# Cross-attention energies split to high and low float16 in SBUF and turned by DMA transposes instead of TensorE, with new instruction orders

## What is computed

```python
x = layernorm(x + causal_attention(x))        # 16 heads of 32
query = ctx @ Wq.T + bq                       # ctx (4, 512, 256), 128 wide
key = ctx @ Wk.T + bk
attention = softmax(query @ key.T, axis=-1)   # (512, 512) for each batch
x = layernorm(x + einsum('bln,bmn->blm', x, attention))
x = layernorm(x + ternary_gated_ffn(quantised(rms_norm(x))))   # hidden 2048
```

## Time and profile before

| | us |
|---|---|
| median of 3 runs | 647.17 (646.59 to 647.51) |
| span of the profiled execution, its own time from first to last instruction | 649.9 |
| TensorE busy | 610.3 |
| VectorE busy | 527.2 |
| ScalarE busy | 417.9 |
| GpSimd busy | 340.8 |

### The profile page before, as it was taken

The page is one execution under the profiler, slowest core; times in us unless marked ns, Lnnn a source line. Parts: engine busy times, 40 slices in busy tenths (PEclk is TensorE's granted clock), DMA queues, the critical chain, the costliest instruction groups (busy, mean ns, idle before and its releaser), DMA issues.

```text
span 649.9 us, 14332 instructions
## 1 busy us (share of the span) xinstructions
PE 610.3 (94%) x5356; PEld 417.1 (64%) x5356; DVE 527.2 (81%) x1376; ACT 417.9 (64%) x789; POOL 340.8 (52%) x472
## 2 busy tenths in 40 slices
...
DMA packets 31461, 45.63 MB, mean 70 GB/s; under 512 B 5664, under 2 KB 22560, under 8 KB 29856
## 3 DMA queue, kind: packets, MB, share of 16 engines
...
...
## 4 chain that ended last, share of the span: by engine, by line
PE 62%; DVE 11%; ACT 6%; issue 4%; SPq 1%; POOL 1%; DMA 1%; POOLq 0%; ACTq 0%; DVEq 0%
PE ps_b L672 20%; PE ps_b L840 15%; PE ps_b L855 14%; PE ps_b L767 4%; PE ps_b L746 3%; PE ps_b L776 2%; DVE ps_b L1118 1%; PE ps_b L729 1%; ACT ph L949 1%; PE ps_b L725 1%; SPq L634 1%; ACT ps_b L950 1%; DVE qk L1100 1%; ACT p L936 1%; DVE dg L1211 1%
## 5 line engine op out<-in xcount | busy, mean ns | idle before, releaser
L1118 DVE CUSTOM_DVE_ANT_0 ps_b<-ps_b,future 128x256 f32<-128x256 f32 (+3 forms) x256 | 118.9, 515 | 17.7 <-PE ps_b L725 11.3
L1319 POOL TENSOR_TENSOR ph<-p,ph 128x512 f16<-128x512 f32 x96 | 110.3, 1165 | 42.2 <-ACT ph L873 41.5
L840 PE MATMUL ps_b<-xqT,sg 128*128 128x256 f16 x1024 | 124.3, 275 | 3.8 <-ACT xqT L873 2.4
L855 PE MATMUL ps_b<-sd,hp 128*128 128x512 fp8e4 x512 | 119.1, 379 | 0.0
L1315 POOL TENSOR_TENSOR hp<-gt,hp 128x512 f16<-128x512 f32 x64 | 74.1, 1164 | 82.7 <-ACT hp L873 82.7
L840 PEld LDWEIGHTS ps_b<-xqT,sg 128*128 128x128 fp8e4 x1024 | 99.4, 98 | 22.5 <-issue 4.1
L1277 POOL TENSOR_SCALAR_AFFINE_SELECT p<-p 128x256 f32<-128x256 f32 (+1 forms) x96 | 46.5, 494 | 77.8 <-ACT p L936 77.0
L672 PE MATMUL ps_b<-xhl,wh 128*128 128x256 f16 x480 | 82.4, 273 | 0.0
L855 PEld LDWEIGHTS ps_b<-sd,hp 128*128 128x128 f16 x512 | 48.7, 98 | 51.1 <-POOL hp L1315 0.3
L1028 ACT ACTIVATE gt<-gt 128x512 f32<-128x512 f32 x64 | 40.1, 629 | 47.0 <-DVE gt L1226 46.9
L936 ACT ACTIVATE p<-ps_b 128x512 f32<-128x512 f32 x96 | 54.2, 598 | 19.3 <-PE ps_b L746 18.5
...
## 6 DMA issues: line engine op xcount, KB each, us to landing
st<-qk SPq DMA_DIRECT2D x192, 64.0 KB, 2.0
...
out_dram<-rows SPq DMA_DIRECT2D x16, 256.0 KB, 2.0
xin<-in_xT_dram SPq DMA_DIRECT2D x14, 256.0 KB, 3.5
...
hp<-in_wT_dram SPq DMA_DIRECT2D x4, 256.0 KB, 4.4
```

The costliest lines, as they stand in the source:

```text
L840: ins = pe.matmul(ps[:, a * HALF:(a + 1) * HALF], sg[:, ("gg", "uu").index(name), c, ht * P:(ht + 1) * P], xqT[:, c, :], start=c == 0, sto ...
L855: ins = pe.matmul(ps[:, :], hp[:, (UNITS * s + n) % HP_SLOTS, h, a, t * P:(t + 1) * P], sd[:, ht, :], start=ht == h == 0, stop=ht == HT - ...
L1118: ins = dve.tensor_tensor_reduce(scores, scores, future[:, S - width:S], 1.0, -3e38, ALU.add, ALU.max, tops[:, g // 2, j:j + 1, g % 2, qt ...
L1319: pool.tensor_tensor(out_, in_, hi, ALU.subtract).then_inc(signal, 1)
```

## The change

`ta` leaves TensorE. A new buffer `ehl` (two slots, high and low, 512 wide, float16) holds the divided energies before they are turned: ScalarE's division writes the high half, VectorE's new `energy_low` the low half from `e32`, the reciprocal and the high half. SP then issues one transposing DMA of both halves of a tile, 128 x 1024 float16, straight into `aT`. The two slots of `ehl` have a semaphore each (`ta_in`); the division of tiles 2 and 3 waits until the transfer of the tile two before it has landed. The wait that protects `aT` from being overwritten (`x2_sum`) moves from ScalarE to SP. The cross product waits for both `ta_in`. `e32` is free when the low half is written. GpSimd's `rms_scale` gets a wait for the root that it reads. `dynamic_dma_scratch_size=4096` is given to the program. All five orders are new; 16 `ta` words leave `PE_ORDER` and `ACT_ORDER` and enter `SP_ORDER`.

```diff
 SP_ORDER = """
+sk0.0.0.1 sk0.0.0.3 sk0.0.1.1 sk0.0.1.0 sk0.0.1.2 sk0.0.1.3 lr0 lx2 lg2 lg3 lr1 ta0.0 sk0.1.0.3 sk0.1.0.0 sh0.0.0
+sk0.1.0.2 sk0.1.0.1 ta0.1 lg4 lg5 sh0.0.1 ta0.2 lx3 lg6 sk0.1.1.0 sk0.1.1.1 sk0.1.1.3 sk0.1.1.2 sh0.1.0 lg7 lg8 ta0.3
+lc1 lg9 lg10 sh0.1.1 lg11 sk1.0.0.2 sk1.0.0.3 sk1.0.0.1 sk1.0.0.0 sk1.0.1.0 sk1.0.1.3 sk1.0.1.1 sk1.0.1.2 lx4 sh1.0.0
+sk1.1.0.3 sk1.1.0.0 sk1.1.0.1 sk1.1.0.2 sh1.0.1 sk1.1.1.2 sk1.1.1.3 ta1.0 ta1.1 sk1.1.1.0 sk1.1.1.1 ta1.2 sh1.1.0 lc2
...
+sk2.1.1.2 ta2.0 sh2.1.0 ta2.1 ta2.2 ta2.3 lc3 zn1.0.0 zn1.0.1 lr4 lx7 sh2.1.1 sk3.0.0.3 sk3.0.0.2 sk3.0.0.1 sk3.0.0.0
...
+ta3.0 ta3.1 sk3.1.1.3 sk3.1.1.1 sk3.1.1.0 sk3.1.1.2 zn2.0.0 zn2.0.1 sh3.1.0 lr6 ta3.2 ta3.3 sh3.1.1 zn2.1.0 zn2.1.1
 PE_ORDER = """
...
+qp qk0.0.3@3 qk0.0.1@1 qk0.0.0@0 qk0.0.2@2 va0.0.0@4 va0.0.1@2 cp0.0@4 cp0.1@3 bv@2 en0.0@3 en0.2@4 mx0.0.0.0@2
+mx0.0.1.0@1 en0.1@0 mx0.0.0.2@5 mx0.0.1.2@6 mx0.0.0.1@3 qk0.1.1@2 mx0.0.1.1@5 mx0.0.3.0@3 mx0.0.3.2@1 qk0.1.0@0
...
+mx0.1.1.1@3 mx0.1.1.4@1 st0.0.1.2@5 mx0.1.1.5@0 qk1.0.0@3 st0.0.2.1@0 st0.0.3.1@1 pv0.0.0.0@6 st0.0.2.2@5 st0.0.3.2@7
+nm0.1.0@4 st0.0.3.0@2 pv0.0.0.1@6 pv0.0.0.2@6 pv0.0.0.3@6 st0.0.2.0@4 pv0.0.1.0@6 pv0.0.1.1@6 pv0.0.1.2@6 pv0.0.1.3@6
+qk1.0.1@4 mx0.1.2.0@6 mx0.1.2.3@2 mx0.1.2.1@5 mx0.1.2.2@0 mx0.1.3.0@3 mx0.1.2.6@6 mx0.1.2.4@5 mx0.1.2.5@1 st0.1.0.2@0
 ACT_ORDER = """
...
+qk0.0.1 qk0.0.2 qk0.0.3 ws3 va0.0.0 wx bv va0.0.1 cp0.0 sg0 cp0.1 xs0.1.0 xs0.1.1 sg1 en0.0 en0.1 ez0.0 qk0.1.0
+qk0.1.1 ez0.1 nm0.0.0 en0.2 qk0.1.2 sg2 qk0.1.3 sg3 va0.1.0 va0.1.1 nm0.0.1 ez0.2 st0.0.0.0 xs1.0.0 xs1.0.1 hi0.0.0.0
+st0.0.0.1 st0.0.0.2 st0.0.1.0 en0.3 st0.0.1.1 hi0.0.0.1 hi0.0.0.2 sg4 st0.0.1.2 hi0.0.1.0 hi0.0.1.1 hi0.0.1.2 sg5
 DVE_ORDER = """
...
+ga0.0.7 mx1.1.1.1 mx1.1.1.2 mx1.1.1.3 hw0.0.7 ta1.0 ta1.1 hd0.0.6 ov1.0.0 hd0.0.7 ez1.2 mx1.1.1.4 ov1.0.1 mx1.1.1.5
+ta1.2 en1.3 mx1.1.1.6 mx1.1.1.7 ez1.3 mx1.1.2.0 mx1.1.2.1 nm1.1.0 mx1.1.2.2 ta1.3 dn0.0.0 mx1.1.2.3 dn0.0.1 mx1.1.2.4
...
+mx3.1.2.6 mx3.1.2.7 mx3.1.3.0 mx3.1.3.1 ta3.2 hd2.1.4 to3.0.0 ta3.3 hd2.1.5 mx3.1.3.2 mx3.1.3.3 lo3.1.0.2 to3.0.1
+op3.0.0 lo3.1.0.3 os3.0.0 op3.0.1 mx3.1.3.4 mx3.1.3.5 tx3.0.0 tx3.0.1 os3.0.1 ga2.1.6 lo3.1.0.5 lo3.1.0.6 hw2.1.6
@@ build
+        ehl = sb("ehl", [P, 2, 2, S], F16)
-        e_inv, e_norm = Signal("e_inv", T), Signal("e_norm", T)
-        ta_hi, ta_lo = Signal("ta_hi", T), Signal("ta_lo", T)
+        e_inv = Signal("e_inv", T)
+        e_hi, e_lo = Signal("e_hi", T), Signal("e_lo", T)
+        ta_in = [Signal(f"ta_in{i}", T // 2 * 16) for i in range(2)]
@@ sync
             def load_context(b):
-                wait(sp, ta_lo, b, 0)
+                wait(sp, e_lo, b, 0)
+            def turn_energies(b, t):
+                wait(sp, e_lo, b, t + 1)
+                wait(sp, x2_sum, 2 * b, 0)
+                sp.dma_start_transpose(aT[:, :, :, t * P:(t + 1) * P].rearrange("p h c m -> p (h c) m"),
+                                       ehl[:, t % 2, :, :].rearrange("p h n -> p (h n)")).then_inc(ta_in[t % 2].sem, 16)
@@ tensor
-            def flip_energies(b, t):
-                wait(pe, e_norm, b, t + 1)
-                flip(("ta", b, t), e32[:, t % 2, :].rearrange("p (c q) -> p c q", c=C))
             def cross(s, t):
-                wait(pe, ta_lo, s // 2, T)
+                for arrived in ta_in:
+                    wait(pe, arrived, s // 2, T // 2 * 16)
@@ scalar
             def energies(b, t):
-                wait(act, ta_lo, b, t - 1) if t >= 2 else wait(act, ta_lo, b, 0)
+                wait(act, e_lo, b, t - 1) if t >= 2 else wait(act, e_lo, b, 0)
             def energy_divide(b, t):
                 wait(act, e_inv, b, t + 1)
-                act.activation(e32[:, t % 2, :], e32[:, t % 2, :], ACT.Copy, scale=erow[:, 1, t:t + 1])\
-                   .then_inc(e_norm.sem, 1)
+                wait(act, ta_in[t % 2], b, t // 2 * 16)
+                act.activation(ehl[:, t % 2, 0, :], e32[:, t % 2, :], ACT.Copy, scale=erow[:, 1, t:t + 1])\
+                   .then_inc(e_hi.sem, 1)
-            def flip_energies(b, t):
-                wait(act, x2_sum, 2 * b, 0)
-                flipped(("ta", b, t), aT, ta_hi)
@@ vector
+            def energy_low(b, t):
+                wait(dve, e_hi, b, t + 1)
+                dve.scalar_tensor_tensor(ehl[:, t % 2, 1, :], e32[:, t % 2, :], erow[:, 1, t:t + 1], ehl[:, t % 2, 0, :],
+                                         ALU.mult, ALU.subtract).then_inc(e_lo.sem, 1)
-                "ta": lambda b, t: flipped(("ta", b, t), aT, ta_hi, ta_lo),
+                "ta": energy_low,
@@ gpsimd
             def rms_scale(s, t):
+                wait(pool, ln_rstd[1], s, t + 1)
@@ kernel
-    nc = bacc.Bacc("TRN2", target_bir_lowering=False, num_devices=1)
+    nc = bacc.Bacc("TRN2", target_bir_lowering=False, num_devices=1, dynamic_dma_scratch_size=4096)
```

More of the change, by code:

```diff
@@ L100 @@
 SP_ORDER = """
[L101 to L110, removed]
+lw0.0 lw0.1 lw0.2 lw1.0 lw1.1 lw1.3 lw0.3 lw1.2 lw2.0 lw2.2 lc0 lw2.3 lw2.1 bi lx1 lw3 sm lg0 lg1 sk0.0.0.2 sk0.0.0.0
@@ L119 @@
[L119 to L143, removed]
```

407 lines of the change are left out of this document (211 added, 196 removed).

## The result

The changed kernel takes 654.26 us (median of 6 runs, 649.51 to 657.83), the kernel before 646.93 in runs on the same chip: ratio 1.0099, 95% interval 1.0072 to 1.0126. It is slower by about 1%: 7.3 us in medians, 6.4 by the ratio. The forecast was 639.2 and its range ended at 653.

A forecast was written before the change was run, and what follows sets the result against it. TensorE's own stream was taken to bound most of the span, ScalarE part of the first batch. TensorE -7.0, ScalarE -2.0, VectorE 0 and transposes +1.0 made -8.0 us, from 647.2 to 639.2 us, range 631 to 653.

The forecast's parts named there:

- the gain is given back: Rival, chance 0.14: the new orders add a 1 us wait in each of 8 half batches, 647 us; with half, 643.
- TensorE -7.0: TensorE loses 16 flips of four transposes, 0.44 us each, mostly where it hardly idles, all counted: -7.0 us.
- ScalarE -2.0: First batch, where ScalarE sets the pace: copies into `aT` go and energy work moves earlier, 2.0 us off the chain.
- VectorE 0: VectorE's 16 subtractions from PSUM become SBUF multiply-subtracts, 693 ns for 686, +0.1 us hidden beside TensorE: 0.
- The transposes +1.0: SP's queue: 16 DMA transposes landing in T = 3.5 us make a batch 1 stack late, +1.0 us counted.
- The rival of a blocked queue: Rival, chance 0.24: transposes hold up batch 1's stacks on SP's queue, deciding from T = 6.0 us; 656 us at 10.3.
- more is won: Rival, chance 0.20: in the first batch half of TensorE's 11 us idle goes, 5.5 us more won, 634 us.

The follow-up runs named there:

- Run 1: The new way of turning (SP's DMA transposes) under all the orders of the kernel before: 649.65 us, 1.0025 of the kernel before.
- run 7: The changed kernel with its new orders only up to about 455 us, then the old ones: 648.23 us, 1.0004 of the kernel before.
- run 8: The changed kernel with its new orders only up to about 520 us, then the old ones: 656.92 us, 1.0148 of the kernel before.
- run 10: Kernel of run 1 with all 16 DMA transposes left out, cross attention reading a constant tile: 647.26 us, 0.9981 of the kernel before.
- run 9: Kernel of run 1 with TensorE's 64 transposes put back at their old places, of a constant, unread: 651.66 us, 1.0052 of the kernel before.
- run 12: Changed kernel with new orders up to about 90 us, then the old, DMA transposes kept, measured again: 646.37 us, 0.9977 of the kernel before.
- run 13: Orders of run 12, but TensorE turns the energies as before, batch 0's turns placed anew: 648.54 us, 1.0002 of the kernel before.
- run 3: Changed kernel with VectorE's low half of the energies replaced by a one-input scaling, subtraction left out: 654.08 us, 1.0084 of the kernel before.
- run 14: Kernel of run 12 with the low half replaced by a one-input scaling, subtraction left out: 645.56 us, 0.9962 of the kernel before.
- run 2: Changed kernel with the 12 DMA transposes of batches 1 to 3 left out, new orders kept: 655.75 us, 1.0115 of the kernel before.

## Why the prediction was wrong

**The step that failed first is the one that had no term: the orders.** The diff rewrites five of them, and the sum priced only the places of `ta`. The rival "the gain is given back" had the mechanism, one wait of 1 us per half batch, but got 0.14 and ended at 649. Behind 120 us TensorE's idle time grew by 14.4 us. Run 1 against the changed kernel puts the price at 4.8 us, and runs 7 and 8 put the main loss into the last part. The rest of the 6.4 us, 1.6, is the new way itself: under the old orders the landing cost 2.8 us (run 10) and the flips gave 1.8 (run 9); the 0.6 left over are within the error. The argument against that rival, 110 us left idle on VectorE, was a mean over the span: VectorE is full in stretches, and in order.

**TensorE -7.0: the spacing was right, the worth was not.** "Mostly where TensorE hardly idles, so I count all of it" failed. The 16 flips do take 7.4 us from start to next start in the kernel before, and TensorE is busy 6.1 us less without them (run 12 for 13). But they were worth 1.8 us (run 9), and the whole exchange of one way for the other 1.6 (runs 12, 13). A stretch in which TensorE is busy 39.8 of 40 us says that TensorE never waits, not that others are ahead of it. The row beside it, VectorE 38.93 of 40, said how near the next bound was.

**ScalarE -2.0: not told apart.** The division kept its length (720 ns for 727), the busy time fell 7.0 us of the 9.7. No run takes out the copies alone; runs 12 and 13 hold them together with the flips, 1.6 us for all. Whether the chain on ScalarE gave 2.0 us stays open.

**VectorE 0: wrong in size, no effect that shows in the time.** 972 ns, not 693: with 686 for the old form, 4.6 us more in all. The row taken as nearest, low halves of the weights, is from the start of the kernel, where GpSimd only fills tiles with a constant; beside its later work the same form is longer (last section). The times of runs 3 and 14 do not tell it from nothing, but in the traces of runs 12 and 14 a part of it is seen as TensorE's pauses.

**The transposes +1.0: T was right (3.2 for 3.5), the place was not.** The rival of a blocked queue needed T over 6 us in batch 1; its first two transfers there landed after 3.3 and 3.2 us. (Two of batch 0 took 8.8 and 7.9, issued at 42.1 and 59.0 us, long ahead of the first cross attention output at 107.1.) The 1.0 us counted for a late stack is there to see, a wait of 1.07 us at 197.0 us, but without the transfers the time was no shorter. In batches 1 to 3 they cost nothing measurable (run 2). The one place where a landing cost time, 2.8 us (run 10), is batch 0 under the old orders, where the last division is just ahead of the cross attention; the new order moved it away.

**The first batch** shrank by 6 us up to 120 us, as the rival "more is won" said, with the lead of 15 us at the first cross attention. But the next batch's context projections (`cp1`) start at 167.2 us in the changed kernel and at 165.9 in run 12, which had no such lead. The range ended at 653 because its slow side was built from one stall alone.

**A version that beats both** came out: the new orders for 90 us, the old for the rest, with DMA transposes: 0.9969 (0.9952 to 0.9987) and 0.9977 (0.9956 to 0.9998) of before, on two chips.
